# Two chunks of sums side by side in one bank instead of three, and one copy for each chunk, in a graph layer with residual and normalisation

## The reference

```python
h_self = x @ W_self.T + b_self
messages = x[src] @ W_neigh.T + b_neigh
h_neigh = segment_sum(messages, dst, num_segments=50000)
y = x + relu(h_self + h_neigh)
out = (y - mean(y)) / sqrt(var(y) + 1e-5)      # over the 128 features
```

## Time and profile before

| | us |
|---|---|
| median of 3 runs | 803.71 (801.73 to 805.24) |
| the profiled execution | 807.21 |
| its span, first to last instruction | 805.3 |
| PE busy | 548.5 (68%) |
| DVE busy | 446.5 (55%) |
| POOL busy | 405.0 (50%) |
| ACT busy | 303.8 (38%) |
| mean granted clock of TensorE | 0.87 of 2.4 GHz |

### The profile page before, as it was taken

How to read it: one execution, slowest core, us unless ns; L and a number is a source line. 1 busy time by engine, 2 the same in 40 slices (tenths; PEclk the granted TensorE clock), 3 DMA queues, 4 the chain that set the end, 5 groups by cost and what they waited for, 6 DMA issues and landing times.

```text
span 805.3 us, 11397 instructions
## 1 busy us (share of the span) xinstructions
PE 548.5 (68%) x3151; PEld 434.5 (54%) x3151; DVE 446.5 (55%) x1927; ACT 303.8 (38%) x789; POOL 405.0 (50%) x424
## 2 busy tenths in 40 slices
PE   1036020118941879889678787888989798999995
PEld 0024010016730657677456576666767576778784
DVE  6783001008821768689566666675645455666765
ACT  0000000015501444446244354435445354566566
POOL 3687777731176556562756566556656566200000
PEclk9999555558985799999879999889979899999998
DMA  4222222113331435444334444434544444433333
GB/s 136 62 63 65 53 52 62 52 27 92 102 83 52 113 103 145 125 129 128 93 93 132 119 122 110 126 110 132 133 110 129 129 126 129 122 109 101 112 107 93
DMA packets 122933, 82.12 MB, mean 102 GB/s; under 512 B 15374, under 2 KB 115894, under 8 KB 122840
## 3 DMA queue, kind: packets, MB, share of 16 engines
q1 hardware_dynamic: 109208, 53.63, 23.5%
q0 software_dynamic: 13664, 27.77, 13.6%
HBM read 55.44 MB, written 26.71 MB: 102 GB/s over the span
## 4 chain that ended last, share of the span: by engine, by line
PE 41%; issue 21%; DVE 15%; another core or an unknown queue 11%; ACT 6%; POOL 4%; DMA 2%; ACTq 1%; DVEq 0%; POOLq 0%
PE bank L889 17%; PE bank L908 8%; PE bank L909 7%; DVE pick L724 4%; PE bank L873 4%; ACT result L1017 3%; PE bank L904 3%; DVE y L735 2%; PE bank L883 2%; DVE stats L755 2%; ACT sums_t L990 1%; POOL ring L462 1%; DMA dst_block<-in_dst,block_index 1%; POOL dst_block L422 1%
## 5 line engine op out<-in xcount | busy, mean ns | idle before, releaser
L462 POOL DMA_INDIRECT ring<-in_x,chunk_src x391 | 379.9, 972 | 265.7 <-issue 110.2
L990 ACT COPY sums_t<-bank 128x496 f32 x131 | 74.9, 572 | 415.5 <-remote 223.1
L889 PE MATMUL bank<-pick,ring 128*128 128x192 f32 (+2 forms) x782 | 227.6, 431 | 2.4 <-DMA ring<-in_x,chunk_src 2.4
L908 PE MATMUL bank<-wsum_t,x_t 128*128 128x128 f32 (+1 forms) x782 | 173.2, 304 | 11.7 <-issue 11.5
L735 DVE SCALAR_TENSOR_TENSOR y<-bank,x_in 128x384 f32<-128x384 f32 x131 | 72.5, 554 | 191.5 <-PE bank L909 73.9
L909 PE MATMUL bank<-wn_t,sums_t 128*128 128x128 f32 (+1 forms) x782 | 158.6, 284 | 19.4 <-issue 19.4
L1017 ACT ACTIVATE result<-y,minus_mean,rstd 128x128 f32<-128x128 f32 x391 | 163.4, 486 | 0.0
L889 PEld LDWEIGHTS bank<-pick,ring 128*128 128x128 f32 x782 | 142.5, 205 | 17.1 <-DMA ring<-in_x,chunk_src 1.9
L908 PEld LDWEIGHTS bank<-wsum_t,x_t 128*128 128x128 f32 (+1 forms) x782 | 124.8, 200 | 37.7 <-issue 37.7
L909 PEld LDWEIGHTS bank<-wn_t,sums_t 128*128 128x128 f32 (+1 forms) x782 | 125.5, 201 | 18.9 <-issue 18.9
L724 DVE TENSOR_SCALAR pick<-columns,local 128x192 f32<-128x192 f32 (+2 forms) x391 | 118.0, 357 | 0.2
(11 more groups left out here) (122 smaller groups left out, 208.8 us busy)
## 6 DMA issues: line engine op xcount, KB each, us to landing
x_in<-in_x SPq DMA_DIRECT2D x130, 192.0 KB
out<-result SPq DMA_DIRECT2D x130, 192.0 KB
ring<-in_x,chunk_src POOLq DMA_INDIRECT x391
degrees_t<-degrees_dram SPq DMA_DIRECT2D x130, 2.2 KB
dst_padded<-in_dst SPq DMA_DIRECT2D x1, 390.6 KB
src_padded<-in_src SPq DMA_DIRECT2D x1, 390.6 KB
edge_src<-in_src SPq DMA_DIRECT2D x1, 390.6 KB
edge_dst<-in_dst SPq DMA_DIRECT2D x1, 390.6 KB
```

The lines of the kernel that those rows point to most:

```text
L462: nc.gpsimd.indirect_dma_start(ring[:, c % RING, :], None, x, bass.IndirectOffsetOnAxis(ap=chunk_src[:, c:c + 1], axis=0)).then_inc(gather ...
L889: ins = mm(sums[:, lo:hi], ring[:, c % RING, :], pick[tau % DEEP][:, PICK_AT[q]:PICK_AT[q] + hi - lo], start=(tau == 0 and q == 0), stop=( ...
L908: mm(h, x_t[b][:, q, 0:rows], k.wsum_t[:], start=False, stop=False)
L990: nc.scalar.copy(sums_t[:, bass.ds(at, SPAN)], sum_bank[tau % SUM_BANKS][:, 0:SPAN]).then_inc(sums_placed, 1)
```

## The change

The bank of a sum now holds two chunks side by side, 192 columns each (`SPAN` = 192, `PAIR` = 2), and there are four such banks; the turned `x` has one bank instead of two. Each chunk has its own offset, its own pick of 194 columns counted from its own first node, and its own copy of 192 columns into `sums_t`. Of the pick the even chunk of a pair uses 193 columns: the last one is the destination that goes on in the odd chunk, and falls into that chunk's first column. From the odd chunk into the next pair the carry matmul stays. Sums are counted by the chunk (`chunks_summed`), and POOL waits by it; the ring has 96 slots. Bounds of drift are 640, 384 and 192 nodes, the look-ahead is `sums_ahead`: two chunks more than needed, in whole pairs. Offsets are loaded eight at a time.

```diff
-SPANS = ((0, 192), (64, 344), (168, 496))
-SPAN = SPANS[-1][1]
-PICK = 800
+SPAN = 192
+PAIR = 2
-DRIFT = 768
+DRIFT = 640
+END_DRIFT = 192
-RING = 84
-SUM_BANKS = 3
-LOAD = 4
+RING = 96
+SUM_BANKS = 4
+LOAD = 8

+def drift_of(chunk):
+    from_end = min(chunk, CHUNKS - chunk)
+    return END_DRIFT if from_end <= END_CHUNKS else TIGHT_DRIFT if from_end <= TIGHT_CHUNKS else DRIFT
+
+def chunks_starting_below(node):
+    return 1 + max(c for c in range(CHUNKS) if P * c - drift_of(c) < node)
+
+def whole_pairs(chunks):
+    return min(CHUNKS, -(-chunks // PAIR) * PAIR)
+
 def sums_needed(trio):
-    return 1 + max(c for c in range(TRIOS) if P * TRIO * c - drift_of(c) < P * TRIO * (trio + 1))
+    return chunks_starting_below(P * TRIO * (trio + 1))
+
+def sums_ahead(trio):
+    return whole_pairs(sums_needed(min(trio, TRIOS - 1)) + PAIR)

 # gather (POOL)
                 if c >= RING:
-                    pool.wait_ge(triples_summed, (c - RING) // TRIO + 2)
+                    pool.wait_ge(chunks_summed, c - RING + 1)

 # spread_lists (DVE)
+                link(v.tensor_tensor(local[:, c0:c1], chunk_dst[:, c0:c1], first_node[:, c0:c1], ALU.subtract))
+                link(v.scalar_tensor_tensor(local[:, r0:r1], carry[:, r0:r1], float(SPAN), local[:, r0:r1], ALU.mult, ALU.max))

 # build_picks (DVE)
                 if tau >= DEEP:
-                    dve.wait_ge(triples_summed, tau - DEEP + 1)
+                    dve.wait_ge(chunks_summed, TRIO * (tau - DEEP + 1))
                 for c in chunks_of(tau):
-                    q = c % TRIO
-                    lo, hi = SPANS[q]
-                    ins = v.tensor_scalar(pick[tau % DEEP][:, PICK_AT[q]:PICK_AT[q] + hi - lo], columns[:, lo:hi],
-                                          local[:, c:c + 1], None, ALU.is_equal)
+                    ins = v.tensor_scalar(pick[tau % DEEP][:, c % TRIO, :], columns[:], local[:, c:c + 1], None, ALU.is_equal)

 # turn_x (PE)
-                if tau >= 2:
-                    pe.wait_ge(xt_copied, tau - 1)
+                if tau >= 1:
+                    pe.wait_ge(xt_copied, tau)

-            def sum_chunks(tau):
-                ...
+            def sum_chunk(c):
+                tau = c // TRIO
+                if c % TRIO == 0:
+                    pe.wait_ge(pick_built, tau + 1)
+                    pe.wait_ge(gathered[tau % GATHER_SEMS], gathers_upto(tau))
+                frame = SPAN * (c % PAIR)
+                into = sum_bank[c // PAIR % SUM_BANKS]
+                carried = 1 - c % PAIR
+                ins = mm(into[:, frame:frame + SPAN + carried], ring[:, c % RING, :], pick[tau % DEEP][:, c % TRIO, 0:SPAN + carried],
+                         start=(c == 0), stop=True, skip_group_check=True)
+                if c % PAIR == 1:
+                    if c // PAIR + 1 >= SUM_BANKS:
+                        pe.wait_ge(sums_placed, PAIR * (c // PAIR + 2 - SUM_BANKS))
+                    ins = mm(sum_bank[(c // PAIR + 1) % SUM_BANKS][:, 0:1], ring[:, c % RING, :], carry[:, c:c + 1], start=True, stop=False, skip_group_check=True)
+                ins.then_inc(chunks_summed, 1)

 # place_sums (ACT)
+                if c % LOAD == 0:
+                    load_offsets(c)
+                at = act.snap(held[c % LOAD], min_val=0, max_val=LAP - 1)
+                if c % PAIR == 0:
+                    act.wait_ge(chunks_summed, min(c + PAIR, CHUNKS))
...
+                    act.wait_ge(sums_placed, c)
...
-                nc.scalar.copy(sums_t[:, bass.ds(at, SPAN)], sum_bank[tau % SUM_BANKS][:, 0:SPAN]).then_inc(sums_placed, 1)
+                frame = SPAN * (c % PAIR)
+                nc.scalar.copy(sums_t[:, bass.ds(at, SPAN)], sum_bank[c // PAIR % SUM_BANKS][:, frame:frame + SPAN]).then_inc(sums_placed, 1)
```

More of the change, by code:

```diff
@@ L235, in build_common_case @@
     degrees = sb("degrees", [SPREAD, COLUMNS, P], BF16)
[L238 removed]
+    expected = sb("expected", [1, CHUNKS])
     gap = sb("gap", [1, CHUNKS])
[L240 removed]
+    faults = sb("faults", [1, 8])
     unused = sb("unused", [1, CHUNKS])
[L244 removed]
+    columns = sb("columns", [P, SPAN + 2])
     ring = sb("ring", [P, RING, DIM])
     x_in = [sb(f"x_in{i}", [P, TRIO, DIM]) for i in range(DEEP)]
[L247 removed]
+    pick = [sb(f"pick{i}", [P, TRIO, SPAN + 2]) for i in range(DEEP)]
     sums_t = sb("sums_t", [P, LAP + MARGIN])
@@ L839, in _ @@
                     clear_lap(cleared_at[t - 1])
-                while built < min(TRIOS, sums_needed(min(t + 1, TRIOS - 1)) + 1):
+                while built * TRIO < sums_ahead(t + 1):
                     build_picks(built)
@@ L874, in turn_x @@
                 ins.then_inc(xt_turned, 1)
-            def sum_chunks(tau):
-                sums = sum_bank[tau % SUM_BANKS]
-                pe.wait_ge(pick_built, tau + 1)
-                if tau >= SUM_BANKS:
-                    pe.wait_ge(sums_placed, tau - SUM_BANKS + 1)
-                if tau:
-                    mm(sums[:, 0:1], ring[:, (tau * TRIO - 1) % RING, :], carry[:, tau - 1:tau], start=True, stop=False, skip_group_check=True)
-                pe.wait_ge(gathered[tau % GATHER_SEMS], gathers_upto(tau))
-                chunks = chunks_of(tau)
-                for c in chunks:
-                    q = c % TRIO
-                    lo, hi = SPANS[q]
-                    ins = mm(sums[:, lo:hi], ring[:, c % RING, :], pick[tau % DEEP][:, PICK_AT[q]:PICK_AT[q] + hi - lo],
-                             start=(tau == 0 and q == 0), stop=(c == chunks[-1]), skip_group_check=True)
-                ins.then_inc(triples_summed, 1)
+            def sum_chunk(c):
[13 more added lines that the diff above has]
+                ins.then_inc(chunks_summed, 1)
@@ L945, in _ @@
                 later_lists(t)
-                while summed < min(TRIOS, sums_needed(t) + 1):
-                    sum_chunks(summed)
+                while summed < sums_ahead(t):
+                    sum_chunk(summed)
                     summed += 1
@@ L1023, in _ @@
             for t in range(TRIOS + 3):
-                while placed < min(TRIOS, sums_needed(min(t, TRIOS - 1)) + 1):
+                while placed < sums_ahead(t):
                     place_sums(placed)
```

104 lines of the change are left out of this document (41 added, 63 removed).

## The result

The changed kernel takes 816.37 us (median of 17 runs, 806.98 to 825.15) against 802.61 us (17 runs) before: a ratio of 1.0134, 95% interval 1.0105 to 1.0164. The ratio leaves out the four executions that lie over 1.5% above the fastest of the changed kernel; the two medians alone give 1.017. It is slower by about 11 to 14 us, where +35 was forecast. The profiled execution took 817.69 us, its span is 815.8 us, 10.5 more than before.

What follows compares the result with a forecast made beforehand. No single engine was taken to bound the kernel throughout; POOL's unbroken gather bursts stall the others. Bursts, quiet trios and earlier gather ends gave +10.6, trios under gathers +24.5: 803.7 + 35.1 = 839 us, own range 812 to 865.

Steps and rivals of the forecast that it cites:

- the mechanism of the loss: Second and third gather bursts: the deeper ring adds 13 gathers to each, +16.2 us each; the first burst +3.8 us.
- PE's saving: PE's sums: fewer columns less half a carry save 0.30 us a trio where PE is the bound, nothing where it waits.
- ACT just keeps up in the quiet trios: Quiet tail: three placing copies cost ACT +1.0 us a trio; 0.1 us of its idle time remains, so PE's saving stands.
- Register loads, picks and the wait of `turn_x` at nothing: Loads of eight offsets, narrower DVE picks and turning's wait for the previous x_t copy: each taken as 0 us.
- ACT's copies under gathers: 70 trios under gathers: ACT's extra 1.0 us on the path every second trio, net +0.35 each, +24.5 us.
- the earlier end of the gathers: Copies 17 to 43 and 45 to 104: the deeper ring lets POOL finish its lists sooner, -6.5 and -8.6 us.
- A: Rival: ACT's path sets the slow stretch, one trio a pause, and the quiet trios' cover is gone; 888 us, chance 0.18.
- B: Rival: bursts are not what stops the others, the second burst's stop has fixed length; 779 us, chance 0.12.
- C: Rival: PE's 0.30 us counts in the slow trios under gathers too; 794 us, chance 0.13.
- D: Rival: no difference, a part of the faster rivals meets a part of the slower one; 804 us, chance 0.08.
- E: Rival: the guard falls to the general branch, costing far more than the kernel itself; under 1%.
- The pace under gathers: Time per trio while POOL gathers: 5.2 us by the forecast, against 4.84 before between copies 45 and 104.

Runs made afterwards that it cites:

- b_split3: Kernel before with its placing copy of 496 columns cut in three, each waiting for the one before: 809.45 us, 1.0077 of the kernel before.
- the rings: Only the ring's slots changed: changed kernel with 84 instead of 96, 792.20 us, 0.9865; kernel before with 96 instead of 84, 831.14 us, 1.036.
- a_wide: Changed kernel with every second chunk's matmul streaming 320 columns instead of 192: 826.34 us, 1.0288 of the kernel before, 1.54% above the changed kernel.

## Why the prediction was right or wrong

- *Direction, and the mechanism of the loss: right, for chips with standstills.* The two long bursts grew with the ring and the others nearly stand through them: +40.1 us where 32.4 was forecast. The size was low: 15 and 16 gathers more, not 13. With the old ring the changed kernel has 35 and 22, 2 and 4 more than before, so the rest of the change, the wait by the chunk and the shorter look-ahead, is worth 2 to 4, not 1, and the twelve slots 12 to 13. That the others "move again when POOL pauses" was too simple: after the first burst they stay nearly still for 14 us more.
- *PE's saving: right.* In the tail the period is in turns 3.83 and 2.96 us, a mean of 3.39 against 3.70, and 3.4 was forecast. The changed kernel's timeline, three bias products in a row:

```profile
702.52 0.33 PE L904 MATMUL bank<-bias,degrees_t 12*128 12x384 bf16 x1
...
706.35 0.33 PE L904 MATMUL bank<-bias,degrees_t 12*128 12x384 bf16 x1
...
709.31 0.33 PE L904 MATMUL bank<-bias,degrees_t 12*128 12x384 bf16 x1
```

- *ACT just keeps up in the quiet trios: right.* Both quiet stretches came within 0.4 us of their forecast. The waits of the changed kernel between 694 and 790 (total us, times, longest) show what its copies wait for; before, it was PE 25 times, 37.5 us in all. ACT's slack of 37.5 has fallen to 15.1, a copy waits for the copy before it only twice, and "issue", where a slow register load would show, ended one wait of 1.1 us:

```profile
ACT sums_t L992 <- PE bank L890: 15.1, 33, 2.7
...
ACT sums_t L992 <- issue: 1.1, 1, 1.1
ACT sums_t L992 <- ACT sums_t L992: 0.3, 2, 0.2
```

- *Register loads, picks and the wait of `turn_x` at nothing:* nothing in the stretches speaks against it, but none was tried by itself.
- *ACT's copies under gathers: wrong, and the step that failed.* "I take +0.35: the extra 1.0 us of ACT on the path every second trio, less 0.15 of what PE saves. That is +24.5". The stretches under gathers came out at -22.5 us, of which -15.1 had been counted for the earlier end of the gathers, so the term was about -7, good to some 7 us only. Measured alone, three copies cost 6.2 us in the whole kernel, at most 8.4. The term let ACT lengthen each restart after a pause of POOL's; the views show that pauses did not lengthen, neither with three copies alone (2.1 us on average) nor in the changed kernel (1.2 us, in place of 2.1, and more of them). The error was in how was read: that ACT's copy is among the first to move after an idle time of 4.07 us does not say that the restart waited for it. The likelier reading is that ACT had been stopped with the rest, and has as much time to spare as they have; no run shows that directly. Why the changed kernel's pauses are shorter is open too. They are so with 84 slots and with PE's columns given back (1.3 and 1.2 us), so neither the ring nor PE's saving makes them; the wait by the chunk, which was not tried alone, is the nearest candidate.
- *How near the total came.* 816 us lies in the forecast's own range, but by parts that offset each other: 32 us too many under gathers, nearly 8 too few in the long bursts. That part is luck.
- *The rivals.* A (888 us, ACT sets the slow stretch) fell with b_split3; B (779, standstills of fixed length) with the rings. C (794, PE's saving counts under gathers too) is made unlikely by a_wide, which gave PE's saving back and lost nothing clear of noise there, with the doubt about the clock. D, parts that cancel, is nearest in time and in kind: -10.8 us against +21.6 for the ring, only not quite equal. E did not occur.
- *The pace under gathers:* forecast 5.2 us, A 5.7, C 4.5. Measured 4.75 (trio 45 to 97, where the gathers end) against 4.85 before (45 to 101).

The parts do not quite sum to the whole. Without its ring the change gives -10.8 us; PE's saving (12.4, from a_wide) and ACT's cost (6.2, from b_split3) make -6.2 and leave -4.6 for the rest: fewer columns in the picks, fewer instructions for the lists, another order of the waits. The three ratios are uncertain by 2 to 4 us each, so it may be nothing; it stays open.

On what the Trainium skill says (Advanced Engine Details and Errata, section The Read-Write Bubble: the memory's latency is exposed between one ScalarE instruction and the next, so tiles should be large): the rows agree in kind. 496 columns take 0.57 us and 192 take 319 ns, so 0.8 ns a column and 0.16 us that are not columns. Cutting one copy in three costs 0.8 to 0.9% of the kernel before on chips of both sorts.

The best version that ran is the changed kernel with 24 slots: 700.43 us on B (two executions), where before takes 809.36, and 0.977 to 0.979 of before on C and D. On D 96 slots give 0.981, with an interval that overlaps. So it is far ahead of both kernels where there are standstills, ahead of the kernel before where there are none, and differs from the changed one in one number.

## What to carry to other kernels

A deeper buffer is not free: it lets its producer run unbroken for longer, and if something in that run stops the others, each slot costs time (1.2 to 1.4 us a slot and burst here). Try the depth by itself, downwards too, before a change that carries it along is credited or blamed. And before an operation is put on the path because it is the first to move after a stop, make that one operation longer; one run tells.

## What the runs showed of the hardware

- The same kernel takes 802 to 809 us on three chips and 581 to 582 us on two. The difference is the standstills that come with unbroken gathers: in 226 to 259 PE of the changed kernel is busy 11.38 us on the one sort and 28.67 on the other, with POOL issuing alike (27 and 25 gathers). What sets them apart, the chips themselves or something of the session, no run here shows. A verdict can hold for one sort only: this change is 1.3% slower on the one and 1.9% faster on the other.
- The standstill does not depend on the bytes gathered: 816.10 us with an eighth of them. It outlives the gathers: in the 14 us after the first burst of the changed kernel PE is busy 0.87, DVE 1.65 and ACT 2.06 us, with POOL at nothing and the DMA engines at 2%.
- Between 408 and 692 PE's granted clock is 0.82 on average in the changed kernel and 0.92 before; on D between 300 and 500, where PE is busy 94% of the time, it is 0.97. In the standstill from 226 to 259 it is 0.51, near the lower level of 1.2 GHz. From run to run the changed kernel's time goes with it only loosely: 806.98 us at a mean of 0.841, 817.69 at 0.804, but 825.15 at 0.810. How much of the clock is cause there, and how much follows from PE's idle time, is open.
